# Letting the five u buffers of a selective scan rotate across batch boundaries

## What is computed

```python
x = _layernorm(x + _L0_attn_ref(x, ...))      # Mamba-like block: projections, convolution, selective scan
x = _layernorm(x + _L0_xattn_ref(x, ctx, ...)) # rmsnorm, projection, weighted sum of a context
x = _layernorm(x + _L0_ffn_ref(x, ...))       # router over 8 experts, two matmuls per expert
```

```python
deltaA  = exp(delta * A)                      # decay
deltaBu = delta * Bm * xc                     # input, called u in the kernel
h = dA * h + dBu                              # the scan over tokens
y = einsum('bdn,bn->bd', h, c)                # product with C, sum over the 16 states
```

## Time and profile before

| | before |
|---|---|
| median of 3 runs | 2643.19 us (2641.14 to 2646.1) |
| span of the profiled execution | 2642.7 us |
| busy: PE, DVE, POOL, ACT | 92%, 79%, 68%, 66% of the span |
| mean granted TensorE clock | 0.955 of full speed |
| first phase (start to the end of batch 15's slots on POOL) | about 1888 us, 16 batches |
| second phase (experts) | the rest |

### The profile page before, as it was taken

How to read it: one execution, slowest core, us unless ns; L and a number is a source line. 1 busy time by engine, 2 the same in 40 slices (tenths; PEclk the granted TensorE clock), 3 DMA queues, 4 the chain that set the end, 5 groups by cost and what they waited for, 6 DMA issues and landing times.

```text
span 2642.7 us, 33255 instructions
## 1 busy us (share of the span) xinstructions
PE 2432.5 (92%) x11291; PEld 2063.5 (78%) x11291; DVE 2085.4 (79%) x2288; ACT 1751.7 (66%) x4011; POOL 1786.3 (68%) x1044
## 2 busy tenths in 40 slices
PE   6788999999999999999999999996869999999997
PEld 6676877878778787877878787775648999999996
DVE  4898999999999999999999999998633444444452
ACT  5667888878888888888888888886543333333331
POOL 1989999999999999999999999999510100000100
PEclk9899999999999999999999999998869999999998
DMA  6042202212021220202112020220142343333420
GB/s 210 8 129 68 84 15 84 72 35 88 19 84 41 66 88 12 91 15 84 51 56 88 12 91 15 77 71 28 59 141 96 130 142 115 112 122 132 141 77 18
DMA packets 90852, 202.62 MB, mean 77 GB/s; under 512 B 7948, under 2 KB 16794, under 8 KB 90702
## 3 DMA queue, kind: packets, MB, share of 16 engines
q1 hardware_dynamic: 81486, 179.21, 20.9%
q0 software_dynamic: 5120, 14.21, 1.7%
q10 hardware_dynamic: 4096, 7.34, 0.9%
HBM read 171.32 MB, written 29.95 MB: 76 GB/s over the span
## 4 chain that ended last, share of the span: by engine, by line
PE 44%; POOL 39%; DVE 8%; issue 6%; DMA 2%; ACT 1%; POOLq 0%; SPq 0%; DVEq 0%; ACTq 0%
POOL arena L969 23%; PE work L1605 12%; PE ring L1605 11%; PE y L1586 8%; POOL arena L974 6%; PE work L1394 5%; POOL arena L980 3%; DVE ring L1261 3%; PE work L1433 2%; POOL arena L901 2%; POOL arena L899 2%; POOL arena L897 2%; DVE arena L1104 1%; DVE arena L1270 1%; POOL expert_rows L930 1%
## 5 line engine op out<-in xcount | busy, mean ns | idle before, releaser
L969 POOL TENSOR_TENSOR arena<-arena 128x896 f32<-128x896 f32 x512 | 1058.0, 2088 | 64.0 <-PE y L1586 55.5
L817 ACT ACTIVATE ring<-arena,small 128x224 f32<-128x224 f32 x2048 | 794.7, 436 | 154.8 <-DVE arena L1270 121.2
L1586 PE MATMUL y<-arena,cst_sb 128*128 128x224 f32 x3584 | 774.9, 368 | 101.0 <-POOL arena L980 69.5
L1261 DVE TENSOR_TENSOR_SCAN ring<-ring,arena 128x896 f32<-128x896 f32 x400 | 809.3, 2023 | 61.5 <-POOL arena L969 41.6
L1586 PEld LDWEIGHTS y<-arena,cst_sb 128*128 128x128 f32 x3584 | 695.7, 198 | 173.9 <-POOL arena L980 78.0
L993 POOL DMA_INDIRECT out<-res,ids x32 | 46.8, 1461 | 640.2 <-DVE mst L1318 542.1
L1270 DVE TENSOR_TENSOR arena<-ring,arena 128x896 f32<-128x896 f32 x400 | 433.4, 1083 | 6.0
L1394 PE MATMUL work<-arena 128*128 128x224 f32 x2000 | 426.3, 371 | 11.0 <-DVE arena L1059 6.0
L1394 PEld LDWEIGHTS work<-arena 128*128 128x128 f32 x2000 | 399.1, 202 | 24.1 <-DVE arena L1104 8.6
L1333 DVE SCALAR_TENSOR_TENSOR hidden_lo<-work,hidden_hi 128x448 fp32r<-128x448 f32 x128 | 79.9, 624 | 346.2 <-ACT hidden_hi L867 346.2
L867 ACT ACTIVATE hidden_hi<-work 128x448 fp32r<-128x448 f32 x128 | 69.7, 544 | 370.6 <-PE work L1605 370.6
(11 more groups left out here) (208 smaller groups left out, 3308.3 us busy)
## 6 DMA issues: line engine op xcount, KB each, us to landing
weights<-in_w SPq DMA_DIRECT2D x64, 1024.0 KB, 7.3
arena<-bc_rows SPq DMA_DIRECT2D x128, 448.0 KB, 4.4
arena<-in_ctx SPq DMA_DIRECT2D x16, 896.0 KB, 5.7
expert_rows<-x2e SPq DMA_DIRECT2D x1, 7224.0 KB, 29.7
xrow<-expert_rows SPq DMA_DIRECT2D x8, 903.0 KB, 11.4
arena<-in_xT SPq DMA_DIRECT2D x16, 448.0 KB, 6.4
arena<-in_x SPq DMA_DIRECT2D x16, 448.0 KB, 3.7
out<-arena ACTq DMA_DIRECT2D x32, 224.0 KB, 2.3
```

Source lines behind the costliest of these rows:

```text
L817: last = nc.scalar.activation(decays[s % 2][:, i * L:(i + 1) * L], delta[:, k, :], ACT.Exp, scale=a_neg[:, n:n + 1])
L969: nc.gpsimd.tensor_tensor(u[:, u_of[s]], dx[:, k:k + 1, :].to_broadcast([P, QN, L]), bc[:, 0, q * QN:(q + 1) * QN, :], ALU.mult).then_inc( ...
L1261: nc.vector.tensor_tensor_scan(states, h, u_flat[:, u_of[s], :], 0.0, ALU.mult, ALU.add).then_inc(scan_done, 1)
L1586: last = nc.tensor.matmul(o, ident, u[:, u_of[s], i, :], start=False, stop=(q == Q - 1 and i == QN - 1), skip_group_check=True)
```

## The change

The buffer of a slot is now given by its number in the whole program, `(b * 32 + s) % 5`, and not by its number in the batch. Each slot therefore uses the buffer of the slot five before, across the batch boundary too, and waits for exactly that one. Everything that names a u buffer takes the batch as well. No instruction is added or taken away, and none changes its place or shape.

```diff
-    u_of = [s % 5 if s < 20 else s % 4 for s in range(SLOTS)]
+    u_of = lambda b, s: (b * SLOTS + s) % UB
...
-                    last = max((p for p in range(s) if u_of[p] == u_of[s]), default=max(p for p in range(SLOTS) if u_of[p] == u_of[s]) - SLOTS)
-                    need(pool, sum_done, b * SLOTS + (last + 1))
+                    need(pool, sum_done, b * SLOTS + s - UB + 1)
...
-                    nc.gpsimd.tensor_tensor(u[:, u_of[s]], dx[:, k:k + 1, :].to_broadcast([P, QN, L]),
+                    nc.gpsimd.tensor_tensor(u[:, u_of(b, s)], dx[:, k:k + 1, :].to_broadcast([P, QN, L]),
...
-                    states = u_flat[:, u_of[s], :] if s in POOLED else h
-                    nc.vector.tensor_tensor_scan(states, h, u_flat[:, u_of[s], :], 0.0, ALU.mult, ALU.add).then_inc(scan_done, 1)
+                    states = u_flat[:, u_of(b, s), :] if s in POOLED else h
+                    nc.vector.tensor_tensor_scan(states, h, u_flat[:, u_of(b, s), :], 0.0, ALU.mult, ALU.add).then_inc(scan_done, 1)
```

More of the change, by code:

```diff
@@ L973, in main @@
                         pool.wait_ge(scan_done, b * SLOTS + (s - 1))
-                        nc.gpsimd.tensor_tensor(u[:, u_of[s - 2]], u[:, u_of[s - 2]], bc[:, 1, q * QN:(q + 1) * QN, :], ALU.mult
+                        nc.gpsimd.tensor_tensor(u[:, u_of(b, s - 2)], u[:, u_of(b, s - 2)], bc[:, 1, q * QN:(q + 1) * QN, :], ALU.mult
                                                 ).then_inc(pooled_ready if s - 2 not in ADDED else multiplied, 1)
@@ L979, in main @@
                         product_made(pool, b, s - 3)
-                        nc.gpsimd.tensor_tensor(u[:, u_of[s - 2]], u[:, u_of[s - 2]], u[:, u_of[s - 3]], ALU.add
+                        nc.gpsimd.tensor_tensor(u[:, u_of(b, s - 2)], u[:, u_of(b, s - 2)], u[:, u_of(b, s - 3)], ALU.add
                                                 ).then_inc(pooled_ready, 1)
@@ L1269, in product @@
                     dve.wait_ge(scan_done, g)
-                    nc.vector.tensor_tensor(u[:, u_of[s]], h.rearrange("p (n l) -> p n l", n=QN), bc[:, 1, q * QN:(q + 1) * QN, :],
+                    nc.vector.tensor_tensor(u[:, u_of(b, s)], h.rearrange("p (n l) -> p n l", n=QN), bc[:, 1, q * QN:(q + 1) * QN, :],
                                             ALU.mult).then_inc(p_ready, 1)
@@ L1585, in main @@
                     for i in range(QN):
-                        last = nc.tensor.matmul(o, ident, u[:, u_of[s], i, :], start=False, stop=(q == Q - 1 and i == QN - 1),
+                        last = nc.tensor.matmul(o, ident, u[:, u_of(b, s), i, :], start=False, stop=(q == Q - 1 and i == QN - 1),
                                                 skip_group_check=True)
```

## The result

The first five runs of the changed kernel have a median of **2626.66 us** (2621.9 to 2638.48), beside 2643.58 us (2641.14 to 2646.1) of before: a ratio of 0.9951, 95% interval 0.9929 to 0.9972. By these five runs it is faster, where I had forecast 2658 us and slower.

What follows compares the result with a forecast made beforehand. PE (44%) and POOL (39%) were taken to hand each other the chain; shorter batches would meet more clock falls, 1500.9 us against 1485.0 over 13 lengths, +15.9 on 2642.7: forecast 2658 us, range 2634 to 2668.

Steps and rivals of the forecast that it cites:

- The slot 21 kind and the slot 9 kind: Batches where POOL waits long for PE at slot 21 alone (114.88 us) or slot 9 alone (113.59 us).
- Steps 1 and 2: Slot 30's wait for PE goes, 0.49 us; the logarithm before line 897 then lets POOL come only 0.40 us earlier.
- Steps 3 and 4: Slot 3's reload wait grows up to 0.40 us, but DVE's first scan gets the 0.40 first, moving place one earlier.
- place one: PE's narrow logits matmuls ahead of slot 9, where a clock fall makes slot 9 wait; forecast 0.40 us earlier.
- place two: PE's narrow rank matmuls ahead of slot 21; gain about 0.28 us, bounds 0 and 0.40, where slot 9 had not waited.
- Steps 5 and 7: Slot 4's new wait for slot 31 of the batch before costs nothing; new addresses cost nothing, within 0.03 us a slot.
- Step 6: Slot 3's 1.73 us reload wait swallows the gain at batch 15; removing slot 29's 1.46 us wait gives nothing.
- The direct sum: Of the 14 boundaries before batch 14, 11 give 0.40 us each: 4.4 us, bounds 0 and 6.9.
- both kinds: Batches with long waits at slots 9 and 21 both, 116.03 us each, forecast for 9.5 of 13 lengths: +15.9 us.
- T: The start of slot 30 in one batch, from which the prediction measured clock falls and batch lengths.
- the mix as now: Rival: the mix of batch kinds stays, so only the 4.4 us counts: 2638.8 us; chance 0.22.
- the slot 9 kind alone: Rival: falls miss the matmuls before slot 21, so 13 batches last 113.19 us: 2629.7 us; chance 0.12.

Runs made afterwards that it cites:

- addresses_only: Kernel before given the rotating buffer addresses but keeping its old waits (slots 24 to 31 and 0 to 3 for the slot four before): 2642.79 us, ratio 0.9991.
- slot30_four: Changed kernel, but slot 30 again waits for the slot four before: 2640.52 us (10 runs), ratio 0.9986.
- after_zeros_five: Changed kernel plus zero-adding matmuls in PE's idle time at slots 4, 14 and 13, and three more ahead of slot 5's sum: 2620.09 us, ratio 0.9924.

## Why the prediction was wrong

**What bounds the kernel.** Right in that POOL and PE hand the chain to each other. Wrong in the sentence "Only the wait at slot 30 is at a slot with four buffers". In batches 0 and 1 slots 25 and 26 wait too, and in batch 0 slot 31. I had read the timeline of steady batches only, though 48 waits and 55.5 us could have been added up. "The slot 21 kind and the slot 9 kind alternate, with one batch of both" passes over batch 5, which has no fall at all and lasts 113.00 us. In batch 1 before shows:

```profile
266.48 2.09 POOL L969 TENSOR_TENSOR arena<-arena 128x896 f32<-128x896 f32 x1 [1.40 <-PE y L1586]
269.14 4.14 POOL L969 TENSOR_TENSOR arena<-arena 128x896 f32<-128x896 f32 x2 [0.57 <-PE y L1586]
```

**Steps 1 and 2** hold: line 897 comes 1.03 us behind the logarithm (1189.08 - 1188.05), the price I had from the earlier trace rows. In batch 0 the gain is small, though not nil: line 897 starts 170.49 - 63.20 = 107.29 us behind the first slot, before 170.12 - 62.69 = 107.43. In batch 1 it is not nil, since there the waits above went and the logarithm came earlier with them.

**Steps 3 and 4** hold: the reload's wait stands at slot 3 in all 15 batches from 1 on, and the first scan waits 0.71 (forecast: about 0.7). Of the 0.40 a batch whose place one binds gets all: 116.44 became 116.03, 113.59 became 113.14 to 113.19. One bound by place two gets 0.03 by the means of 13 and 6 batches (114.90, now 114.87), give or take 0.2: nearer to my lower bound of 0 than to the 0.28. **Steps 5 and 7** hold: no wait stands at slot 4, and the addresses were measured by themselves. **Step 6** is not contradicted: POOL's wait at slot 29 is gone, but with the clock held up the stretch from slot 0 of batch 15 to the end is 863.4 and 865.7 us in the changed kernel's two traces and 862.5 and 866.9 in before's.

**The direct sum** was 4.4 us, and measured with the clock up it is 5.1. It came close by luck, by two errors that cancel: 1.9 us in batch 1 were missing, and the steady batches without a fall give 0.26, not 0.40.

**The step that failed is the clock's**: "The falls that now give slot 9 alone (+37.70) go beyond the boundary to both", and from it "most of batches 3 to 14" of both kinds, 9.5 of 13, for +15.9 us. Batches of 116.02 to 116.04 us are 0 of 12 in the first trace of the changed kernel and 4 of 36 in three; the whole time went down by 8.3 us in the mean. The lengths by kind of fall, batches 2 to 13; left three traces with the waits of before in steady batches (before, addresses_only, slot30_four), right three of the changed kernel (their times average 2631.0 us, 4.3 below the mean of its 29 runs, so they flatter it). A long fall lasts 6.8 us, a short one 3.4:

| falls in the batch | as before: count, length | changed: count, length |
|---|---|---|
| long, place one | 15, 113.53 to 113.72 | 2, 113.14 to 113.19 |
| long, place two | 13, 114.79 to 115.18 | 6, 114.69 to 115.17 |
| long at both | 3, 116.44 to 116.45 | 4, 116.02 to 116.04 |
| short at both | 1, 112.77 | 12, 112.07 to 114.06 |
| short, place one | 1, 111.98 | 3, 111.79 to 112.00 |
| none | 3, 112.68 to 113.23 | 4, 111.60 to 112.97 |
| others | 0 | 5, 112.89 to 115.67 |
| mean length | 114.18 | 113.51 |

The pattern of both kinds exists, lasts 116.03 us as worked out, and repeats itself as argued. But it is narrow. It holds for falls from about +25.49 (before's batch 9) to +25.55; I let it go on without an end beyond +25.49. Past it, from +25.57 to +27.2, lie the cheapest batches of the changed kernel with a fall, of 111.8 to 112.8 us for most. The edge could have been read from the trace of before: its batch 14 has the fall at 1689.52, +25.61 behind slot 0 (1663.91) and +37.97 behind T, later than the latest I used, and is 113.35 us long from T to T, with a wait of 1.39 at slot 17 and none at slots 9 and 21.

```profile
1651.55 2.09 POOL L969 TENSOR_TENSOR arena<-arena 128x896 f32<-128x896 f32 x1 [0.49 <-PE y L1586]
...
1764.90 2.09 POOL L969 TENSOR_TENSOR arena<-arena 128x896 f32<-128x896 f32 x1 [0.49 <-PE y L1586]
```

```profile
1689.00:1690.00 1.00, 1.00 (x10) 1.00 (x9) 1.00 (x2) 1.00 (x3) 1.00 (x1) 0.76 0.00 0
```

**Which rival was nearest.** In number, the mix as now, 2638.8 us, beside a mean of 2635.3. Its mechanism is not what happened: the mix is another one (short falls at both places in 12 batches instead of one, a long fall in 13 instead of 31), and only its cost came out much alike. That the first median of 2626.66 us lies near the 2629.7 of *the slot 9 kind alone* is chance: that kind stands 2 times in 36. Over 29 runs the mean clock is within 0.001 of before's (0.9566 and 0.9562). That says that the time at 1.2 GHz is nearly the same, and not that it costs the same, since short falls cost less than long ones (last section). What an execution takes goes with where its falls stand: within each set of 12 runs of the changed kernel the time goes with the clock, by about 2.0 us for each 0.001. Of the 8.3 us, about 5 are shown to be direct. The other 3 lie within the 3.3 of uncertainty, and 0.0004 of clock at that slope would account for 0.8 of them; whether the mix is a little cheaper stays open. My argument that three runs within 5 us showed a steady mix was weak too: 99 runs of before lie between 2631.09 and 2652.69.

The Trainium skill (TensorE: Matmul & The Clock Gate, "What's actually happening") says that the clock's monitor is free-running and does not reset when a kernel starts, so that the same kernel can be caught at another phase. Three traced executions of the same program with three sequences of falls, and 29 runs of it from 2620.71 to 2650.42 us, agree. The same section of the Trainium skill puts the ramp penalty below 1% of a typical kernel's span and advises not to fit a model to a specific count of slow matmul instructions. That advice did better than my fit. The size is no reason to leave the clock out here: keeping it up took 24 us of 2644, 0.9%, off before, with the added work's own cost already paid and short falls still left, and single runs of the changed kernel differ by 29.7 us, 1.1%. That is more than the whole 0.3% of the change.

## What to carry to other kernels

Where a profile shows the clock falling in steady batches, first find what a change gives with the clock held up: add matmul instructions that count for nothing, no longer than the idle time they stand in, to both versions, and compare those. Do not forecast from one trace which falls a shorter batch will meet; batches whose falls lay 0.02 us apart differed by 3.4 us, and one execution has only a dozen of them. Give such a kernel 20 runs or more before a difference of half a per cent is believed (the same pair gave 14.6 us in one set and 4.8 in the next), check in the rows by how much an added instruction really holds its engine up, and add up all the waits of a line, first and last batches too, before saying which of them a change removes.

## What was unexpected

Falls of 3.4 us at 1.2 GHz cost far less than half of what falls of 6.8 us do: short ones at both places gave batches of 112.07 to 112.77 us in most cases, against 111.82 for none with the added work, and long ones at both 116.03. And a batch can settle on its own fall, at a dear length (four times 116.03) or at a middling one (eight times 112.65 in after_zeros_five). What makes the length of a fall 3.4 or 6.8 us was not tried.
